# Dense bf16 products of constants on TensorE at nine points of its order, in a fused embed, scan, mixture-of-experts and attention kernel

## What is computed

```python
h = tok(x); h = concatenate([h, txt(x_txt, mask)], axis=1)
h = h + scan(layernorm(h))            # per token: 3-vectors rotated, scaled, added up along the sequence
h = h + moe0(layernorm(h))            # router, top 2 of 8 experts, 192 -> 288 -> 192, gelu
h = h + linear_attention(layernorm(h))  # relu(q), relu(k), 12 heads
h = h + moe1(layernorm(h))            # router, top 2 of 8 experts, 192 -> 768 -> 192, silu
```

## Time and profile before

| | us |
|---|---|
| median of 3 runs | 477.72 |
| lowest and highest of the 3 | 477.71, 478.19 |
| time of the profiled execution | 477.29 |
| its span, first to last instruction | 475.5 |
| PE busy in it | 388.3 (82%) |
| DVE, POOL, ACT busy | 277.6, 221.4, 170.4 |
| mean granted TensorE clock | 0.894 of full |

### The profile page before, as it was taken

How to read it: one execution, slowest core, us unless ns; L and a number is a source line. 1 busy time by engine, 2 the same in 40 slices (tenths; PEclk the granted TensorE clock), 3 DMA queues, 4 the chain that set the end, 5 groups by cost and what they waited for, 6 DMA issues and landing times.

```text
span 475.5 us, 8082 instructions
## 1 busy us (share of the span) xinstructions
PE 388.3 (82%) x2467; PEld 320.2 (67%) x2467; DVE 277.6 (58%) x1304; ACT 170.4 (36%) x350; POOL 221.4 (47%) x265
## 2 busy tenths in 40 slices
PE   4797768887426999999659889228999999999992
PEld 4543535645424888888547779217999999999992
DVE  3889999799782445445395258873444534334320
ACT  1189976361560111111135105462233232332320
POOL 3400389998025677775300002334656555555432
PEclk9688769999755999999859999757999999999997
DMA  8439000000042122221299900492233232323222
GB/s 250 64 88 240 3 0 3 1 33 2 12 143 58 59 76 76 84 77 58 82 323 306 309 11 2 108 126 78 42 58 49 50 60 40 48 52 49 41 25 26
DMA packets 38044, 38.18 MB, mean 80 GB/s; under 512 B 7546, under 2 KB 34158, under 8 KB 38002
## 3 DMA queue, kind: packets, MB, share of 16 engines
q1 hardware_dynamic: 26486, 22.13, 18.8%
q0 software_dynamic: 9312, 14.03, 15.0%
q10 hardware_dynamic: 2204, 1.49, 1.1%
HBM read 27.28 MB, written 10.37 MB: 79 GB/s over the span
## 4 chain that ended last, share of the span: by engine, by line
PE 51%; DMA 18%; DVE 15%; ACT 9%; issue 5%; POOL 1%; POOLq 0%; SPq 0%; DVEq 0%; ACTq 0%
PE bank L1843 14%; DMA out<-reg,idxs 12%; PE bank L1802 7%; PE bank L1817 5%; PE bank L1821 3%; DMA xn_rows<-gate 2%; PE bank L2039 2%; DVE bank L1226 2%; PE bank L1829 2%; DVE reg L1219 2%; ACT reg L794 2%; PE bank L1885 2%; DMA con<-in_consts 2%; PE bank L1788 2%; PE bank L2001 1%
## 5 line engine op out<-in xcount | busy, mean ns | idle before, releaser
L1843 PE MATMUL bank<-reg 128*128 (+1 forms) x558 | 105.7, 335 | 1.4 <-DVE reg L1465 0.7
L1843 PEld LDWEIGHTS bank<-reg 128*128 128x128 f32 (+1 forms) x558 | 90.0, 191 | 12.0 <-issue 8.0
L686 POOL DMA_INDIRECT out<-reg,idxs x31 | 49.0, 1581 | 61.5 <-DMA out<-reg,idxs 29.9
L672 POOL DMA_INDIRECT reg<-xn_rows,idxs x62 | 60.8, 981 | 30.9 <-issue 15.7
L1476 DVE TENSOR_SCALAR reg<-bank,gs 128x192 f32<-128x192 f32 x31 | 12.9, 417 | 84.1 <-PE bank L1843 84.1
L959 ACT ACTIVATE reg<-bank 128x384 f32<-128x384 f32 x31 | 15.2, 490 | 100.3 <-PE bank L1821 97.2
L1817 PE MATMUL bank<-xTs,xT 128*128 128x128 f32 x372 | 48.0, 280 | 0.0
L1817 PEld LDWEIGHTS bank<-xTs,xT 128*128 128x128 f32 x372 | 45.2, 196 | 0.4 <-DVE xTs L1451 0.4
L680 POOL DMA_INDIRECT expert_rows<-reg,idx x31 | 30.6, 987 | 19.1 <-DVE reg L1474 12.7
L955 ACT ACTIVATE reg<-bank 128x288 f32<-128x288 f32 x31 | 12.7, 410 | 72.9 <-PE bank L1802 72.9
L1226 DVE TENSOR_REDUCE bank<-reg 128x6 f32<-128x24 f32 x272 | 37.7, 184 | 0.2 <-issue 0.2
(11 more groups left out here) (349 smaller groups left out, 753.3 us busy)
## 6 DMA issues: line engine op xcount, KB each, us to landing
reg<-in_w2b SPq DMA_DIRECT2D x8, 576.0 KB, 8.9
reg<-in_w1b SPq DMA_DIRECT2D x8, 384.0 KB, 9.0
reg<-in_w1a SPq DMA_DIRECT2D x8, 216.0 KB
reg<-in_w2a SPq DMA_DIRECT2D x8, 216.0 KB
xn_rows<-xn SPq DMA_DIRECT2D x4, 384.0 KB, 2.7
reg<-in_w1b SPq DMA_DIRECT2D x16, 96.0 KB, 7.7
xn_rows<-xn SPq DMA_DIRECT2D x1, 1152.0 KB, 8.5
out<-h SPq DMA_DIRECT2D x1, 1152.0 KB, 12.5
```

Of the source, the lines that this page charges most:

```text
L672: pool.indirect_dma_start(xs[:, i % RING, 0:(D, D2)[l]], None, xd[l], bass.IndirectOffsetOnAxis(ap=idxs[:, i:i + 1], axis=0)).then_inc(xs_ ...
L686: pool.indirect_dma_start(out, bass.IndirectOffsetOnAxis(ap=idxs[:, i:i + 1], axis=0), ys[:, i % RING, :], None, compute_op=ALU.add).then_ ...
L1843: ins = MM(bank[6][:, 0:D], (hTs if l == 0 else hT2[:, p])[0:r, c * P:(c + 1) * P], w2v[0:r, bass.ds(e * (nhc * D) + c * D, D)], start=(c ...
```

## The change

A helper `keep_busy(n, bk)` issues n products of a constant with a constant: 128 bf16 columns as stationary operand (64 float32 columns of the identity, read as bf16), 512 bf16 columns as the moving one (the first 256 float32 columns of `con`), into all of PSUM bank `bk`. Nothing reads these results, and they carry no semaphore. Six calls, three of which run for both layers, make nine groups, 142 products in all, with a wait for all `pair_ready` in front of the first:

```diff
+            def keep_busy(n, bk):
+                for _ in range(n):
+                    MM(bank[bk][:, :], con[:, 0:P // 2].bitcast(BF16), con[:, 0:2 * P].bitcast(BF16), start=True, stop=True)
...
             def ranks(l):
+                keep_busy((24, 28)[l], 2)
                 pe.wait_ge(msk_ready, l + 1)
...
+                keep_busy((16, 14)[l], 2)
                 pe.wait_ge(oneB_ready, l + 1)
...
                 ins.then_inc(inv_mm, 1)
+                keep_busy(16, 7)
...
+            pe.wait_ge(pair_ready, 7)
+            keep_busy(5, 7)
             logits()
+            keep_busy(5, 7)
             pe.wait_ge(ld_idw, 16)
...
             ins.then_inc(bias_mm, 1)
+            keep_busy(18, 6)
             t_pair(3, 0)
```

## The result

The changed kernel takes 472.34 us in the median of 4 runs (471.26 to 473.23), the kernel before 477.72 on the same chip (476.48 to 478.19): 0.9908 of the time, interval 0.9885 to 0.9931. Its profiled execution took 472.83 us with a span of 471.0, the mean granted clock rose from 0.894 to 0.944. The forecast was 471.4 in 469.6 to 475.2.

A forecast was written before the change was run, and what follows sets the result against it. Engines ahead of PE set its waits, but experts(0), attention and experts(1) do bound work at half clock. Gains of 0.1 + 0.2 + 3.0 + 1.5 + 1.5 = 6.3 us gave a median of 471.4 us, range 469.6 to 475.2.

The forecast's parts named there:

- Price of a product: Each 512-column product put in takes 0.43 us at clock 0.50 and 0.215 at 1.00, at most 0.51 and 0.26.
- Do they fit?: All groups fit PE's waits at the high clock; most are too long at the low, but dense products should lift it.
- Logits and states: At the logits and L2001: ten products cost nothing, and a higher clock under L2001 gains 0.1 us, at most 0.4.
- Counts and inversion: In ranks(0) and ranks(1): faster counts gain 0.2 us for both layers, since DVE and the gates' transfer set the pace.
- Experts(0): At the start of experts(0): the high clock gains 3.0 us, with 4.4 as upper bound and 0 to 1.2 from below.
- rival D: All stages: everything holds, a gain of 7.6 us, so 470.1 us; chance 0.12.
- Rival A: The clock falls again ahead of both expert stages, leaving a gain of 2.3 us, so 475.4 us; chance 0.16.
- Attention: From attention's first transposes to the second kv group: 1.5 us gained, bounds 0 and 1.8, limited by ACT's normed rows.
- Experts(1): At the start of experts(1): faster L1817 and transposes gain 1.5 us, 1.7 at most, 0 at least.
- The end: Last scatter: whatever comes earlier at the first scatter comes earlier at the end, taken whole, if the scatters keep their pace.
- B (no effect): The products fit but do not hold or lift the clock anywhere: 477.7 us; chance 0.04.
- C (overrun): The products do not lift the clock and delay the counts and stages, costing 5.2 to 9.6 us, some 485; chance 0.08.

The follow-up runs named there:

- without the 16s: The changed kernel without its two groups of 16 products behind the inversions: 476.58 us, ratio 0.9996 to the kernel before.
- without the 18: The changed kernel with only the two groups of 16 behind the inversions, all other groups left out: 471.07 us, ratio 0.9889 to the kernel before.
- with 8 columns: The changed kernel with all 142 products in place, each of 8 columns instead of 512: 477.78 us, ratio 1.0025 to the kernel before.
- the repetition: The changed kernel timed and profiled again, with no edit: 470.53 us, ratio 0.9885 to the kernel before.
- the late groups alone: The changed kernel with only 16 and 16 products behind the inversions and 18 ahead of attention: 469.22 us, ratio 0.9862; on another chip 486.09 us, 0.9899.
- with 21 products: The changed kernel, all groups kept, with 21 in place of 16 products ahead of experts(0): 471.02 us, ratio 0.9878 to the kernel before.
- the run with 32: The late groups alone, with 32 in place of 16 products behind the first inversion: 474.07 us, ratio 0.994 to the kernel before.
- the group in the scan: The late groups alone plus 15 products and a wait ahead of the scan's assembly: 468.41 us, ratio 0.983; on another chip 485.65 us, 0.9888.
- the early groups only: The changed kernel with only 5, 5, 24, 28, 16 and 14 products at logits, counts and one-hot rows, on another chip: 489.25 us, ratio 0.9986.

## Why the prediction was right, and where it was not

**What bounds the kernel** was read rightly. The time from the states to the end is set by DVE, POOL and the transfers at the four waits, and by PE at three stage starts; where the clock was changed at those three, time came back, elsewhere at most 0.24 us a place. The runs without the 16s, without the 18 and with 8 columns show that it is the clock, by 512-column work right ahead of the stage. Of the signs that the prediction named, one failed in part: behind the four waits clock 1.00 was to stand from the first product, and the counts of the first layer ran at 0.50.

**Price of a product.** 0.43 and 0.215 were taken, with 0.51 and 0.26 as the other end. The rows give 0.42 at the low clock (15 in 6.37) and 0.22 to 0.23 at the high one (15 in 3.40, 21 in 4.70), by whose difference six products take 1.30 us, 0.217 each. The Trainium skill's figures, 426.7 and 215.7 ns from start to start ("TensorE: Matmul & The Clock Gate", section "Wait — 56ns, not 53.3ns?"), agree with these rows.

**Do they fit?** Yes, in this execution, ahead of the waits that matter. "A stream that starts low should lift the clock itself", after 3 to 7 us, held nearly: the clock rose 2.6 to 4.2 us into the groups of the kernel with the late ones and 6.1 into that ahead of the scan. The groups that the text found "too long" at the low clock are so at times, as the repetition's 16 ahead of the one-hot rows, without a cost there.

**Logits and states**, 0.1: 0.02 (5.72 us in place of 5.74), since L2015 still had 0.50 in its first half. In the repetition the clock was up all through it, and its timeline and stretch read

```profile
117.52 5.50 PE L2015 MATMUL bank<-reg 128*128 128x144 f32 x24 [0.79 <-DVE reg L1287]
```

```profile
117.60:123.20 5.60, 5.60 (x26) 5.43 (x27) 3.73 (x24) 2.22 (x4) 0.00 (x0) 1.00 0.01 1
```

That is 0.24 us for the whole half at the low clock, and as much at the counts (13.17 behind the states, not 13.41). The bound of 0.4 and the reading that this line hardly follows the clock hold. By the Trainium skill's rule for weight loads ("TensorE: Matmul & The Clock Gate", section "LDWEIGHTS (loading the stationary operand)"), as the prediction worked it out, the line would have halved; no run here shows that. (The 2.5 us that the prediction gives for it don't come out of its rows: half of 5.74 is 2.9.) What paces it may be the weight loads all the same: the earlier trace rows has PEld busy for 2.80 of 2.80 us of it and for 2.29 of 2.50, and a load of this line takes 292 to 333 ns in the kernel before, where the rule's figure is 107. No run tested this.

**Counts and inversion**, 0.2: 0.02 in layer 0, 0.24 in layer 1 (the one-hot rows start that much sooner behind the counts). In layer 0 the counts ran at 0.50, as the clock fell at 131.6 after 2.5 us of idling behind the group of 23 records. The 0.87 us that the first gathered rows of experts(1) come sooner is not of this term: it is there with 8 columns too (8.11), and in all other profiles (8.0 to 8.3). The profile of before was the odd one, through the gates' transfer, 10.82 us where it is 9.43 in the changed kernel and 7.7 to 8.3 in the others looked at.

**Experts(0)**, 3.0: the step that failed. Measured 1.18 + 1.15 = 2.33. The sum took as given that the clock holds through the thin part, with bounds of 4.4 and "0 to 1.2" if it does not. What came was between: the clock fell, but only behind the first g1, and was back at 152.1 in place of 156.1. The rows price it: g1 2.13 in place of 1.14, t_h 0.88 for 0.53, t_x 0.66 for 0.39, together 1.6, nearly the difference of *e0* between the changed kernel and the late groups alone (5.79 and 4.12). With the clock up, first rows to bias products takes 82.39 us in place of 86.49, 4.1 less; 0.4 of it is lost as these 16 overrun, so that 3.7 are left from the counts on, the 3.7 of rival D. The reason was in the text, in the wrong place. Rival A named the thin part, and said against it that the groups "last longer if they start low, which closes the gap". That was right, but the prediction did not go on to see that the early groups make sure that this one starts high. It counted the early groups as free; counted from the counts on they cost this term 1.3 us (2.4 in place of 3.7). Or the group has to be longer behind them: with 21 products the term is 3.8.

**Attention**, 1.5: 1.13 here, 1.49 and 1.48 with the late groups alone on two chips. The term was sized well; 0.35 was lost at the second transposes' wait for ACT's normed rows, the chain that the prediction named. But attention also starts 0.48 later behind the bias products, and from these to the second kv group the gain is 0.65 us here and 1.08 in the repetition, where the late groups alone have 1.66. A likely part of this: the clock fell 0.2 to 0.3 us into the bias products in both profiles (230.6, 229.5), and DVE could read the last of them (L1514) 3.8 and 3.9 us behind the first, in place of 2.7; before, it fell behind them, at 234.6. It isn't the whole of it, as with 21 products attention starts 9.91 behind the bias products with L1514 at 2.2; the ten remaining profiles have 9.3 to 9.7. The cause was not tested.

**Experts(1)**, 1.5: 1.62, and 1.62 to 1.68 in the other profiles with the 16 products on these chips (1.42 and 1.45 on the one where the kernel before takes 490.55). The group there starts at the low clock and reaches to the rows. By the prediction's own sign, a wait for the first rows that is gone, it overran, but by next to nothing: the rows come 8.12 behind the one-hot rows, and 8.13 in the run without this group. The 1.62 is too small, though, because the profile of before was lucky there. Its rows came late, its clock rose 4.7 us behind the first transposes, and *e1* was 8.19; in the three other profiles that enter this stage cold the clock rose 5.6 to 5.9 us behind them, and *e1* was 8.55 to 8.69. From the one-hot rows to the first g2 these three take 16.7 to 16.8 us and the changed kernel 14.69, so the clock is worth 2.0 to 2.1 us, and of the 0.87 only some 0.4 is chance on top.

**The end.** "As long as the scatters keep their pace" was the condition. They did not by 1.78 us in the first profile, and did but for 0.67 in its repetition. The terms from the table come to 2.33 + 1.13 + 0.24 + 1.62 + 0.04 = 5.4 us, or 5.8 with experts(1) taken against the cold profiles; the medians gained 5.38, and 6.2 in the repetition. The forecast of 6.3 was right in sign and size. How close it came is in part luck: the term for experts(0) was 0.7 too high and that for experts(1) some 0.5 too low, and runs of one kernel differ by 2 to 3 us. The profiled pair gained only 4.46, with 0.46 and 0.87 won and 0.48 and 1.78 lost outside the terms.

**The rivals.** B (no effect) is what products of 8 columns do. C (overrun) did not happen; the run with 32 shows that it would be paid nearly in full, 3.71 us at the first rows and 3.49 at the first scatter. A happened in part, in one stage. D, a gain of 7.6 us, was reached with fewer products, not more: 7.5 with the late groups alone, and 8.2 with the group in the scan as well; on the chip where everything takes longer the same two gained 4.5 and 4.9.

## What to carry to other kernels

In this kernel, work that only lifts the clock paid where the engine's next work was bound by that clock, and hardly elsewhere (50 products gained 7.5 us, the 92 others nothing clear of noise). Look for such places, put dense products there alone, and size them so that they end where the real work begins, at the clock at which they will in fact start: too short, and the clock falls in the gap; too long, and nearly each microsecond is paid. An earlier group that makes this one start fast makes it end early, and opens the gap in which the clock falls. Where a chain of transfers sets the end, repeat the profile before you explain the last microseconds of a ledger.

## What the runs showed of the hardware

- 142 products of 8 columns left the clock at 0.50 at the stage starts, where as many of 512 columns at the same places brought 1.00.
- The clock also fell inside a dense stretch, some time behind an idle part: at 148.6, 4 us after the products, while PE was in g1, and at 276.1 and 278.3 behind 1.5 us of idle time, there in 3 of 11 profiles (290.8 in the third). Each cost 1.6 to 1.7 us. Such stretches may be much of the spread of 2 to 3 us between runs: with 21 products the three runs around 469.3 us have a mean granted clock of 0.954 and the three around 472.7 one of 0.943. Where in an unprofiled run the clock was low isn't on record.
- Scatters that wait for each other's landing have odd ones of 5.3 to 7.1 us between starts, two to five in a stage, where 4.2 to 4.6 is usual. First to last took 137.1 to 139.5 in thirteen profiles of kernels with the same code there. What makes them slow isn't known.
- On one chip all kernels took some 14 us more, nearly all of it in experts(0) between its first g2 and the bias products: 92.7 to 94.1 us where it is 78.3 to 79.7 elsewhere. The waits of DVE in the kernel with the early groups only show there, for four of its 31 copies of a result (L1474):

```profile
DVE reg L1474 <- remote: 12.0, 4, 3.1
```

This row, a wait that ends with something from outside the core's own engines, is missing in the profiles of the other chips; the two other profiles of this chip have it for five and eight copies (15.4 and 24.6 us). That it is a slower landing of the scatters of that stage is a guess, and wasn't tested. Gains are smaller in microseconds there (4.5 in place of 7.5 for the late groups); part of that is that its clock also fell twice inside experts(0), at 184.1 and 218.2.
